# Output stage: beta added to the residual rows on GpSimd, the first normalization ended in one VectorE pass

## The reference, cut to what matters

```
n     = layernorm(x);  ctx = attention(n, ctx_2048, mask)      # 16 heads of 64
delta = clip(residual_scale, 0, 0.3) * (ctx @ Wo.T + bo)
delta = (delta - mean) / sqrt(var + 1e-5) * ln_gamma + ln_beta
x1    = x + delta
h2    = layernorm(x1)
out   = x1 + moe(h2)                                           # 64 experts, 8 a token
```

## Time and profile before

| | us |
|---|---|
| three timed runs, median (lowest to highest) | 6567.19 (6564.72 to 6573.34) |
| the profiled execution's own time | 6554.6 |
| its span | 6553.0 |
| PE busy in the span | 6387.5 (97%) |
| DVE busy | 3695.7 (56%) |
| ACT busy | 2889.1 (44%) |
| POOL busy | 2123.3 (32%) |
| output stage, from its first instruction to its last | 2269.5 to 2801.7 |

### The profile page before, as it was taken

One profiled execution on the slowest core, in us unless ns is written; L12 is line 12 of the kernel. 1 busy time (PEld: TensorE's weight loads), 2 busy tenths in 40 slices (PEclk: granted clock), 3 DMA queues, 4 the chain that ended last, 5 costly groups with the idle time before them and its releaser, 6 DMA issues.

```text
span 6553.0 us, 105959 instructions
## 1 busy us (share of the span) xinstructions
PE 6387.5 (97%) x31978; PEld 5666.8 (86%) x31979; DVE 3695.7 (56%) x4618; ACT 2889.1 (44%) x3319; POOL 2123.3 (32%) x1887
## 2 busy tenths in 40 slices
PE   9999998999999999879999999999999999999998
PEld 7888887887888788779989999999899999999997
DVE  5443434999999889835454454443533444444444
ACT  3222224888888744424343343332422333333333
POOL 1010000000000145544444454444444444444444
PEclk9999999999999999989999999999999999999999
DMA  8754565555555577557676776665755566666666
GB/s 281 242 193 148 149 148 145 129 130 127 128 128 126 150 195 170 137 122 196 157 215 167 187 198 168 169 169 111 193 113 111 140 140 169 143 164 168 157 160 164
DMA packets 844890, 1049.59 MB, mean 160 GB/s; under 512 B 440705, under 2 KB 638081, under 8 KB 844802
## 3 DMA queue, kind: packets, MB, share of 16 engines
q0 software_dynamic: 123984, 368.70, 25.4%
q1 hardware_dynamic: 564432, 382.50, 23.7%
q10 hardware_dynamic: 156386, 297.29, 13.3%
HBM read 725.85 MB, written 322.31 MB: 160 GB/s over the span
## 4 chain that ended last, share of the span: by engine, by line
PE 48%; DMA 3%; issue 2%; DVE 2%; POOL 1%; ACT 1%; DVEq 0%; ACTq 0%; POOLq 0%; SPq 0%
PE moe_ps_gate L1394 5%; PE moe_ps_gate L1396 5%; PE moe_ps_gate L1395 5%; PE moe_ps_up L1396 5%; PE moe_ps_up L1395 5%; PE moe_ps_up L1394 5%; PE moe_ps_y L1383 5%; PE moe_ps_y L1382 5%; PE moe_ps_y L1381 5%; PE moe_ps_hT L1401 1%; DMA moe_tokens<-h2st,moe_rows 1%; DMA first_raw<-in_w_up 1%; DVE moe_gu_lo L1502 1%; POOL moe_tokens L1336 1%; DMA out<-moe_y,moe_rec_s 1%
## 5 line engine op out<-in xcount | busy, mean ns | idle before, releaser
L1336 POOL DMA_INDIRECT moe_tokens<-h2st,moe_rows x1156 | 1256.4, 1087 | 1902.2 <-DVE moe_rows L1512 1633.8
L1394 PE MATMUL moe_ps_gate<-moe_gu_hi,moe_xT_hi 128*128 128x384 f32 x2288 | 794.2, 347 | 67.8 <-DVE moe_xT_lo L1506 51.4
L1525 DVE SCALAR_TENSOR_TENSOR moe_hidden<-moe_hidden,moe_rec_w,moe_ps_up 128x384 f32<-128x384 f32 x286 | 175.6, 614 | 1150.7 <-PE moe_ps_up L1396 963.0
L1395 PE MATMUL moe_ps_gate<-moe_gu_lo,moe_xT_hi 128*128 128x384 f32 x2288 | 767.8, 336 | 0.0
L1396 PE MATMUL moe_ps_gate<-moe_gu_hi,moe_xT_lo 128*128 128x384 f32 x2288 | 767.6, 335 | 0.0
L1394 PE MATMUL moe_ps_up<-moe_gu_hi,moe_xT_hi 128*128 128x384 f32 x2288 | 765.0, 334 | 0.6 <-DVE moe_gu_lo L1502 0.6
L1395 PE MATMUL moe_ps_up<-moe_gu_lo,moe_xT_hi 128*128 128x384 f32 x2288 | 764.6, 334 | 0.0
L1396 PE MATMUL moe_ps_up<-moe_gu_hi,moe_xT_lo 128*128 128x384 f32 x2288 | 764.5, 334 | 0.0
L1430 ACT CAST moe_xT_hi<-moe_ps_turned 128x1024 fp32r<-128x1024 f32 x287 | 291.2, 1015 | 905.0 <-PE moe_ps_up L1396 708.2
L1383 PE MATMUL moe_ps_y<-moe_d_hi,moe_hT_lo 128*128 128x512 f32 x1722 | 676.5, 393 | 0.0
L1382 PE MATMUL moe_ps_y<-moe_d_lo,moe_hT_hi 128*128 128x512 f32 x1722 | 675.0, 392 | 0.0
(11 more groups left out here) (207 smaller groups left out, 13742.0 us busy)
## 6 DMA issues: line engine op xcount, KB each, us to landing
first_raw<-in_w_gate ACTq DMA_DIRECT2D x63, 1536.0 KB
first_raw<-in_w_up ACTq DMA_DIRECT2D x63, 1536.0 KB
moe_raw_d<-in_w_down ACTq DMA_DIRECT2D x63, 1536.0 KB
proj_a_raw<-in_ctxT POOLq DMA_DIRECT2D x64, 512.0 KB, 5.7
kst<-proj_o SPq DMA_DIRECT2D x256, 128.0 KB, 2.8
vst<-proj_o SPq DMA_DIRECT2D x64, 512.0 KB, 2.6
qst<-proj_o SPq DMA_DIRECT2D x256, 128.0 KB, 2.2
att_kt<-kst SPq DMA_DIRECT2D x64, 512.0 KB
```

Source lines behind the costliest of these rows:

```text
L1336: nc.gpsimd.indirect_dma_start(out=tokens[:, g * (H // G):(g + 1) * (H // G)], out_offset=None, in_=h2_quarters, in_offset=bass.IndirectOf ...
L1394: nc.tensor.matmul(o[:, 0:I], xT_hi[:, c], gu_hi[:, b, k, c], start=(c == 0), stop=False)
L1395: nc.tensor.matmul(o[:, 0:I], xT_hi[:, c], gu_lo[:, b, k, c], start=False, stop=False)
```

## The change

GpSimd adds beta to the residual rows in place, `x_t = x_t + beta`, once for each tile (`add_beta`). VectorE waits for that (`xb_done`) in place of the load, and line 1040 writes `x1` itself; line 1045 and the wait in front of it are gone. The wait for the store of the buffer `x1` (`stored`) now stands in front of the pass that writes `x1`.

On GpSimd the first three adds stand behind the wait of line 886 and a wait for the constants; each later one stands in front of the scatter of the tile three before it. With an even number of tiles the last scatters are written out behind the loop.

```diff
+                def add_beta(i, b, nth):
+                    pool.wait_ge(x_in[b], 16 * nth)
+                    pool.sem_inc(pool_passed, 1)
+                    nc.gpsimd.tensor_tensor(x_t[:, b], x_t[:, b], beta_sb[:], ALU.add).then_inc(xb_done, 1)
+
+                pool.wait_ge(consts_in, 16 * CONSTS)
+                add_beta(0, 0, 1)
+                add_beta(1, 1, 1)
+                add_beta(2, 0, 2)
+                with pool.Fori(0, NT // 2 - 2) as h:
+                    add_beta(2 * h + 3, 1, h + 2)
                     scatter(2 * h, 0)
+                    add_beta(2 * h + 4, 0, h + 3)
                     scatter(2 * h + 1, 1)
+                add_beta(NT - 1, 1, NT // 2)
+                for j in range(NT - 4, NT):
+                    scatter(j, j % 2)
...
-                NORM_STEPS = 2 * (HV + 1) + 2
+                NORM_STEPS = 2 * (HV + 1) + 1
...
-                    dve.wait_ge(x_in[b], 16 * nth)
-                    nc.vector.scalar_tensor_tensor(out=scaled[:], in0=scaled[:], scalar=rstd[:, 0], in1=x_t[:, b],
-                                                   op0=ALU.mult, op1=ALU.add).then_inc(norm_step, 1)
-                    dve.wait_ge(norm_step, NORM_STEPS * i + HV + 3)
+                    dve.wait_ge(xb_done, i + 1)
                     if not (known(i) and i < 2):
                         dve.wait_ge(stored[b], 32 * nth - 32)
-                    nc.vector.tensor_tensor(x1[:, b], scaled[:], beta_sb[:], ALU.add).then_inc(x1_done, 1)
+                    nc.vector.scalar_tensor_tensor(out=x1[:, b], in0=scaled[:], scalar=rstd[:, 0], in1=x_t[:, b],
+                                                   op0=ALU.mult, op1=ALU.add).then_inc(x1_done, 1)
```

More of the change, by code:

```diff
@@ L763, in output_pass @@
         shift_done = s.sem("shift_done")
+        xb_done = s.sem("xb_done")
         t_done, h2T_done, logits_done, diff_done, e8_done = s.sem("t_done"), s.sem("h2T_done"), s.sem("logits_done"), s.sem("diff_done"), s.sem("e8_done")
@@ L894, in scatter @@
                             in_=record[:, b, k, :], in_offset=None).then_inc(scattered[b], 16)
-                with pool.Fori(0, NT // 2) as h:
+                def add_beta(i, b, nth):
[8 more added lines that the diff above has]
+                    add_beta(2 * h + 3, 1, h + 2)
                     scatter(2 * h, 0)
+                    add_beta(2 * h + 4, 0, h + 3)
                     scatter(2 * h + 1, 1)
+                add_beta(NT - 1, 1, NT // 2)
+                for j in range(NT - 4, NT):
+                    scatter(j, j % 2)
                 for b in range(2):
@@ L1038, in normalize @@
                     dve.wait_ge(norm_step, NORM_STEPS * i + HV + 2)
-                    dve.wait_ge(x_in[b], 16 * nth)
-                    nc.vector.scalar_tensor_tensor(out=scaled[:], in0=scaled[:], scalar=rstd[:, 0], in1=x_t[:, b],
-                                                   op0=ALU.mult, op1=ALU.add).then_inc(norm_step, 1)
-                    dve.wait_ge(norm_step, NORM_STEPS * i + HV + 3)
+                    dve.wait_ge(xb_done, i + 1)
                     if not (known(i) and i < 2):
                         dve.wait_ge(stored[b], 32 * nth - 32)
-                    nc.vector.tensor_tensor(x1[:, b], scaled[:], beta_sb[:], ALU.add).then_inc(x1_done, 1)
+                    nc.vector.scalar_tensor_tensor(out=x1[:, b], in0=scaled[:], scalar=rstd[:, 0], in1=x_t[:, b],
+                                                   op0=ALU.mult, op1=ALU.add).then_inc(x1_done, 1)
                     dve.wait_ge(x1_done, i + 1)
-                    moments(i, 1, x1[:, b], HV + 3, (lambda: context_low(i + 2, b)) if more else (lambda: None))
+                    moments(i, 1, x1[:, b], HV + 2, (lambda: context_low(i + 2, b)) if more else (lambda: None))
                     nc.vector.tensor_scalar(shift[:], mv[:, 1, 0:1], rstd[:, 1], -1.0, ALU.mult, ALU.mult).then_inc(shift_done, 1)
```

## The result

The changed kernel takes 6605.98 us (median of 5 runs, 6603.23 to 6611.01), the kernel before, run beside it, 6569.0 us (5 runs, 6564.72 to 6573.34). The ratio is 1.0058, interval 1.0046 to 1.007: 37 us slower. The forecast was 6584 with a range of its own from 6571 to 6597; the direction was right, and the 16.9 us that it added were less than half of what came. The time lies above that range.

The account below looks back on a forecast made before the run. VectorE was taken to bound the output stage at 15.24 us a tile, TensorE close at 14.59. Head +7.0, 29 tiles by 0.34 +9.9, tail 0: 6567.2 + 16.9 = 6584 us, own range 6571 to 6597 (6552 to 6597 with no hold).

Parts of the forecast that it names:

- What bounds: Output stage: VectorE bounds at 15.24 us a tile, TensorE follows at 14.59; writing slot 28 moves the end one for one.
- Removed: VectorE, output stage: 32 passes of line 1045 go, 1.36 us a tile, leaving VectorE alone at 13.88 us.
- The add: GpSimd, output stage: 32 adds of 128x1024, 2.2 us each (1.75 to 2.6), falling into GpSimd's idle gap.
- The hold: Output stage: GpSimd's add and VectorE's two-input passes exclude each other, period 15.6 us, +9.9 us over 29 tiles; forecast's chance 0.48.
- the term s: VectorE's wait at prod for GpSimd's add: 1.7 us a tile on average, 1.3 to 2.1 by the add's length.
- no hold: Rival, output stage: both engines read undisturbed, TensorE bounds at 14.59 us, together -11.7 us, 6555.5; chance 0.30.
- Where the add starts: GpSimd, steady tiles: the add starts at 8.4 or 8.9 us of VectorE's tile, ahead of prod at 9.14.
- Who is held: VectorE, steady tiles: prod, due at 9.14, waits 1.5 or 2.0 us; c_lo runs until 8.4, before the add.
- a longer hold: Rival, VectorE: small passes right behind c_lo are held too, s 2.3 us, period 16.2, 6602 us; chance 0.07.
- The head: Start of the output stage: the first add waits for all fills; loss 5.7 to 7.9 us, taken as 7.0.
- The tail: End of the output stage, from tile 28's scatter on: as long after the change, 0 us.
- From the trace to the median: Whole program: profiled execution from 6554.6 to 6571.5 us, +16.9; timed runs stand 12.6 above it, carried over to 6584.

Follow-up runs that it names:

- the memset: Changed kernel with its first two adds ahead of the fill DMAs, each add then replaced by three GpSimd memsets of 832 columns, beta left out: 6557.15 us, ratio 0.9983.
- the extra add: Kernel before, plus a GpSimd add of gamma and beta into a spare tile for each tile, which nobody waits for: 6647.33 us, ratio 1.0123.
- the missing add: Changed kernel without any GpSimd add, VectorE waiting for the load instead, beta left out: 6567.76 us, ratio 1.0001.
- beta in the projections: Changed kernel without GpSimd adds; VectorE adds beta in the projections, SP stores the rows and the output stage loads them: 6566.61 us, ratio 0.9995.

## Why the prediction was wrong in size

**What bounds.** Right. VectorE alone is 13.88 us where nothing holds it (tiles of 13.88 to 13.91 without the add), TensorE alone 14.53 (predicted 14.59), and the stage's end moved with slot 28.

**Removed.** Right: 1.32 us from pass to moments, 1.36 saved a tile.

**The add.** 2.39 us, predicted 2.2, within the bounds of the earlier trace rows. By the Trainium skill (GPSIMD Engine Reference, Performance versus the Vector engine) 2.25 us had been estimated; the trace has 6% more. The add ends before it is wanted in all tiles but the first, as said.

**The hold: the step that failed.** The mechanism was right: VectorE's passes of two inputs in SBUF (the memory on the chip in which the tiles lie) and the add exclude each other, as the memset, the extra add and the missing add show. The failed step is the term s, the loss to the hold, taken as 1.7 us a tile and measured as 2.17. Two parts of its working were off.

The prediction gave the exclusion two in three, since "one row of 0.18 us is all that there is". The trace of the kernel before held more, in the very DMAs that the earlier trace rows counts. VectorE, then GpSimd:

```profile
2533.60 1.21 DVE L1008 TENSOR_TENSOR out_cn<-ahead_c_raw,ahead_r_t 128x1024 f32<-128x1024 f32 x1
```

```profile
2532.63 0.97 POOL L892 DMA_INDIRECT table<-out_record,out_slot  x1 [0.30 <-issue]
2533.91 1.75 POOL L892 DMA_INDIRECT table<-out_record,out_slot  x1 [0.30 <-issue]
```

A scatter DMA takes 0.97 us; one that starts well within a pass of two inputs ends 0.85 us behind that pass. One as long as this comes in every other tile, 12 times from 2380 to 2740 us, and that is most of the difference between the 10.1 and the 11.0 us. GpSimd waits for VectorE there, and the chance of no hold could have been put far lower.

*Where the add starts.* The prediction put it at 8.4 or 8.9 us of the tile, ahead of `prod` at 9.14, from eight scatter DMAs in 10.1 or 11.0 us. `prod` starts at 9.15 (2436.24 - 2427.09). But the eight DMAs now take 2436.35 - 2425.15 = 11.2 us, and 11.5 in the tile before it, and so the add starts at 9.26: abreast of `prod`, not 0.2 to 0.7 us ahead. Then `prod` loses the whole add. By the prediction's own sum, with 11.2 in place of 10.1 and 11.0: 11.75 + 11.2 - 13.88 = 9.07. It isn't the add that makes them slow, for in the kernel without one the eight take 11.3 to 11.6 us in most tiles. Their length depends on which passes they meet, and the change moved the passes: the 10.1 and 11.0 were taken over from an order that the change undoes.

*Who is held.* `c_lo` at 7.18 was taken to be safe, being done or being first. It is safe only when it is done. In 5 of the 28 tiles from 2330 to 2790 us the DMAs took 10.0 to 10.6 us, the add came 0.53 us behind `c_lo`'s start, and `c_lo` took 4.0 us and not 1.21. In 21 it was `prod` that was held. The prediction's rule was that of the Trainium skill (SBUF — State Buffer, Who interferes with whom): a VectorE instruction with two SBUF inputs contends with a GpSimd instruction that reads SBUF, and the order of issue decides which of them is blocked. The traces agree with the exclusion, 2.48 us for 0.67, and with the order where the lead is clear (0.71 us and more, above). What misleads is the start in a record: by it `prod` at 2436.24, 0.11 us ahead of the add, should have had its 0.68 us and the add some 0.6 us of waiting; `prod` had 3.06 and the add 2.40.

So s is, by the means from 2330 to 2790 us, 2.35 - 0.68 = 1.67 us at `prod` and 1.71 - 1.21 = 0.50 at `c_lo`, 2.17 together, where 1.7 was taken. `prod` alone came out as the 1.7 by luck: 21 tiles of 28, at 2.2 us each. The term lacked `c_lo`. 13.88 + 2.17 = 16.05; the other 0.18 to 16.23 is about the size of VectorE's waits for `d` (2.4 us over the 28 tiles) and for the logits (2.5). Against 15.6 this is 0.63 us a tile, 18 us over 29, nearly all that the forecast lacked. Another 1.5 us came from its base: it set 15.6 against 15.24, two tiles of the earlier trace rows, where the stage's mean is 15.19. The rival of a longer hold, 6602, came nearest, from another mechanism: it had the small passes behind `c_lo` held. That was seen once, at the head of the stage (L1099 at 2324.11 took 1.66 us, in the mean 0.25), and is not what filled the tiles.

**The head.** 10.1 and not 7.0, nor the 7.9 at most of the range. The first add started at 2301.95, 1.6 us behind the 2300.3 that was worked out; and the second add held the pass at once, which had been the upper of two cases.

**The tail.** Nothing was predicted, 4.3 us came in one trace and about 1 in the other.

**From the trace to the median.** 16.9 was predicted; 37 (median), 39 and 46 (the two traces' stages) came.

**The other rivals.** "No hold" fell with `prod`. Its price was wrong too: -17 us for 29 tiles at TensorE's 14.59. The three kernels with nothing that holds VectorE's long passes (memsets, no add, beta in the projections) gave -10, 0 and -1. In their traces VectorE is no longer the bound, and TensorE has stalls of its own, behind some of them the low clock. The prediction took the gap of 0.6 us between two bounds as wholly to be had.

## What to carry to other kernels

Work moved from VectorE to GpSimd is not off VectorE's path if GpSimd reads SBUF while VectorE has a pass of two SBUF inputs: one of the two stands until the other ends, and the trace shows it as a longer duration with no wait. Look first for pairs that the kernel has already: here GpSimd's scatter DMAs of 1.75 us in place of 0.97 told of it. Before such a move, mark GpSimd's new instruction on VectorE's timeline; if a two-input pass starts within its length, or up to about 0.6 us ahead of it, count up to its whole length against VectorE, and compare that with what is removed (here 2.17 against 1.36 us). And where a second engine is 4% behind the bound, a faster first engine may bring nothing: here 1.36 us a tile less on VectorE was worth 0 to 10 us, not the 19 of 29 x 0.66.

## What the runs showed of the hardware that was not expected

- A VectorE pass of two inputs that is held by GpSimd's add ends 1.07 to 1.10 us behind the add's end with 1024 columns and 0.55 to 0.57 with 512, whether its record starts ahead of the add's or behind: `c_lo` about 4.0 us for an add of 2.40; `prod` 3.06 us (0.11 ahead), 2.98 (with it), 2.45 (0.52 behind).
- The other way round, an add that is held ends 2.2 us behind the end of VectorE's pass (2.77 us in all), and a scatter DMA 0.85 us behind it (1.75 us in place of 0.97).
- Record starts don't give the order: behind a scatter DMA the add went first although `c_lo` started 0.54 us ahead of it; with a lead of 0.74 us `scaled` went first.
- GpSimd's memsets of about the same total length hold neither `prod` (0.68 us) nor `c_lo` (1.21).
- In some places a granted clock of 0.50, the 1.2 GHz level, came for 3 to 7 us behind idle times of TensorE of 1 us or so; a matmul of 512 columns then takes 0.63 us and not 0.39. In the kernel before idle times of nearly 1 us left the clock at 1.00.
- VectorE's small dependent instructions at the stage's end came 1.4 us apart in one execution of the changed kernel and 0.2 us apart in the other.
